# Flamingo gated cross attention: the Q projection moved beside K and V, with shorter lags between the stages

## The reference, cut to what matters

```python
q = (hidden_states @ Wq.T).reshape(bsz, q_len, H, HD).transpose(0, 2, 1, 3)
k = (cross_attention_states @ Wk.T).reshape(bsz, kv_len, KVH, HD).transpose(0, 2, 1, 3)
v = (cross_attention_states @ Wv.T).reshape(bsz, kv_len, KVH, HD).transpose(0, 2, 1, 3)
q = _rmsnorm(q, q_norm_w)
k = jnp.repeat(k, GROUPS, axis=1)
v = jnp.repeat(v, GROUPS, axis=1)
k = _rmsnorm(k, k_norm_w)
scale = 1.0 / np.sqrt(HD)
scores = jnp.einsum('bhqd,bhkd->bhqk', q, k) * scale
scores = scores + attention_mask[:, :, :, :kv_len]
probs = jax.nn.softmax(scores.astype(jnp.float32), axis=-1).astype(q.dtype)
out = jnp.einsum('bhqk,bhkd->bhqd', probs, v)
out = out.transpose(0, 2, 1, 3).reshape(bsz, q_len, H * HD)
return out @ Wo.T
...
base = jnp.einsum('bsd,od->bso', x, W) + bias
return base + lora_out
```

## Time and profile before

| | us |
|---|---|
| median of 3 runs (lowest, highest) | 886.33 (886.28, 888.25) |
| span of the profiled execution, first to last instruction | 882.5 |
| what lies around it, median less span | 3.8 |
| busy: PE, PEld | 830.6, 684.3 |
| busy: DVE, ACT, POOL | 605.8, 416.3, 411.8 |

### The profile page before, as it was taken

How to read it: one execution, slowest core, us unless ns; L and a number is a source line. 1 busy time by engine, 2 the same in 40 slices (tenths; PEclk the granted TensorE clock), 3 DMA queues, 4 the chain that set the end, 5 groups by cost and what they waited for, 6 DMA issues and landing times.

```text
span 882.5 us, 15501 instructions
## 1 busy us (share of the span) xinstructions
PE 830.6 (94%) x4592; PEld 684.3 (78%) x4592; DVE 605.8 (69%) x1710; ACT 416.3 (47%) x1271; POOL 411.8 (47%) x484
## 2 busy tenths in 40 slices
PE   4888889769999999999999999999999999999897
PEld 3555556438888888888888888888888888888786
DVE  5789999633666666676666666666766667666995
ACT  3344444323654455455545545554555455445431
POOL 2566776643553255336435532553363355335532
PEclk9899999889999999999999999999999999999999
DMA  7401000010110011001101100110012010100011
GB/s 262 147 24 30 31 24 13 0 49 24 39 58 25 1 49 61 13 0 48 71 0 48 48 24 0 48 59 12 0 48 71 0 48 24 48 1 13 0 38 59
DMA packets 16947, 34.34 MB, mean 39 GB/s; under 512 B 2320, under 2 KB 2448, under 8 KB 16656
## 3 DMA queue, kind: packets, MB, share of 16 engines
q1 hardware_dynamic: 16912, 33.91, 11.9%
HBM read 31.80 MB, written 2.10 MB: 38 GB/s over the span
## 4 chain that ended last, share of the span: by engine, by line
PE 71%; DVE 3%; issue 2%; POOL 1%; ACT 0%; DVEq 0%; POOLq 0%
PE bank L1122 19%; PE bank L1124 18%; PE bank L1123 18%; PE bank L1210 5%; PE bank L1136 4%; PE bank L1163 3%; PE bank L1138 2%; DVE score L1316 1%; PE bank L1218 1%; POOL rq L1005 1%; PE bank L1226 0%; POOL rk L1001 0%; ACT prob L1050 0%; PE bank L1236 0%; POOL probn L994 0%
## 5 line engine op out<-in xcount | busy, mean ns | idle before, releaser
L994 POOL TENSOR_TENSOR probn<-prob,erec 128x512 f32<-128x512 f32 x64 | 66.8, 1043 | 252.0 <-PE bank L1163 222.4
L1077 ACT ACTIVATE qT_hi<-bank 128x512 fp32r<-128x512 f32 x64 | 38.3, 599 | 161.9 <-PE bank L1124 161.9
L1122 PE MATMUL bank<-nT_hi,wq_hi 128*128 128x512 f32 x256 | 105.2, 411 | 1.8 <-POOL ones L960 1.8
L1122 PE MATMUL bank<-wo_hi,oT_hi 128*128 128x512 f32 x256 | 105.0, 410 | 0.4 <-DVE wq_raw L1373 0.4
L1050 ACT ACTIVATE prob<-score,nmax 128x128 f32<-128x128 f32 x256 | 99.6, 402 | 9.9 <-DVE nmax L1321 9.8
L1124 PE MATMUL bank<-nT_hi,wq_lo 128*128 128x512 f32 x256 | 102.1, 399 | 0.0
L1123 PE MATMUL bank<-nT_lo,wq_hi 128*128 128x512 f32 x256 | 101.9, 398 | 0.0
L1124 PE MATMUL bank<-wo_hi,oT_lo 128*128 128x512 f32 x256 | 100.9, 394 | 0.0
L1123 PE MATMUL bank<-wo_lo,oT_hi 128*128 128x512 f32 x256 | 99.7, 389 | 0.0
L1005 POOL TENSOR_TENSOR rq<-qss,neghalf 128x4 f32<-128x4 f32 x64 | 65.1, 1017 | 50.3 <-DVE qss L1387 50.3
L1381 DVE TENSOR_SCALAR knat<-bank,rk 128x128 f32<-128x128 f32 x64 | 22.4, 350 | 95.4 <-POOL rk L1001 95.4
(11 more groups left out here) (192 smaller groups left out, 2191.8 us busy)
## 6 DMA issues: line engine op xcount, KB each, us to landing
wq_raw<-in_wq SPq DMA_DIRECT2D x32, 256.0 KB, 3.6
wo_raw<-in_wo SPq DMA_DIRECT2D x32, 256.0 KB, 3.0
wkv_raw<-in_wkv SPq DMA_DIRECT2D x8, 512.0 KB, 3.6
ctxn<-in_ctx_n SPq DMA_DIRECT2D x8, 256.0 KB, 2.7
ctxt<-in_ctx_t SPq DMA_DIRECT2D x8, 256.0 KB, 2.7
out<-wkv_raw SPq DMA_DIRECT2D x8, 256.0 KB, 2.0
xres<-in_x SPq DMA_DIRECT2D x1, 1280.0 KB, 11.3
wbase<-in_wbase SPq DMA_DIRECT2D x1, 1024.0 KB, 8.2
```

What stands on the lines that cost most here:

```text
L994: pool.tensor_tensor(probn[:], prob[:], erec[:].unsqueeze(2).broadcast_to([P, HG, P]), ALU.mult).then_inc(normed, 1)
L1077: act.activation(qT_hi[:, s % HG, first * P:(first + 4) * P], q_bank[:], ACT.Copy).then_inc(q_h, 1)
L1122: pe.matmul(out, l_hi, r_hi, start=start, stop=False)
```

## The change

Q is projected token-major too, one batch at a time, with the turned x as the stationary operand and the four heads' weights as the moving one (`project_qkv`), into the PSUM bank beside K and V, so that one tile holds four heads of Q, K and V. ACT squares Q and K together (640 columns), DVE sums them along the row, POOL makes the five inverse norms, DVE scales Q and K together, and PE turns five tiles (`turn_qk`) instead of one. The one-column products and `rq` go; the mask is added and the two score parts are added in one DVE operation each. Per batch there is one slot, with the projection 2 ahead, the turn 1 ahead, probabilities 1 behind and the output projection 2 behind; its addition to x is 3 behind and stands first in DVE's list. The tiles of the cast Wq, Wk and Wv weights are doubled, so that heads alternate. The last stage moves: `fold` stands behind the scores; STAT, NORM and TURN are slots 59, 60 and 62 for batch 0; `turn_batch` and `feed_forward` of one batch stand in the same slot, and `add_batch` stands first in DVE's list of the next. The input wq is laid out accordingly. The loop body has 16 slots. Removed functions are in the listing above; of the new ones these matter:

```diff
-    LAG = 4
     N = G * B
-
-    WQ_SLOT = {2: (0,), 3: (1,), 4: (2,), 5: (3,)}
-    WO_SLOT = {1: (0, 1, 2, 3)}
-
-    LOW_SLOT = {0: (0,), 2: (1,), 3: (2, 3)}
+    RING = 4
+    WKV_AT = 0
+    WQ_AT = {2: (0,), 3: (1,), 4: (2,), 5: (3,)}
+    FOLD = N - B
+    STAT, NORM, TURN = N - B + 3, N - B + 4, N - B + 6
+    LAST = TURN + B - 1
...
+        wkv_hi = wkv_hi + [sb(st, "wkv_hi1", [P, CH * 2 * P], F32R)]
+        wkv_lo = wkv_lo + [sb(st, "wkv_lo1", [P, CH * 2 * P], F32R)]
+        wq_hi = wq_hi + [sb(st, f"wq_hi{c}", [P, D], F32R) for c in range(1, 2 * CH)]
+        wq_lo = wq_lo + [sb(st, f"wq_lo{c}", [P, D], F32R) for c in range(1, 2 * CH)]
...
+        s_bank = pair[0][:].rearrange("p (h i t) -> p h i t", h=HG, i=2)
+        q_bank = bank[2]
+        kv_bank = pair[1][:, HG * P:(HG + 2) * P]
+        qk_bank = pair[1][:, 0:(HG + 1) * P].rearrange("p (h t) -> p h t", h=HG + 1)
+        v_bank = pair[1][:, (HG + 1) * P:(HG + 2) * P]
+        kt_bank = pair[1][:, (HG + 2) * P:(HG + 3) * P]
+        qt_bank, pt_bank, o_bank, y_bank = bank[4:8]
+        t_bank, f_banks = bank[2], (bank[3], bank[4])
...
+        def loops(eng, slot):
+
+            for s in range(-2, B):
+                slot(0, s)
+            with eng.Fori(0, G // 2 - 1) as i:
+                for s in range(B, 3 * B):
+                    slot(i, s)
+            for s in range(N - B, LAST + 2):
+                slot(0, s)
...
+                def project_qkv(i, s, n):
+                    even = parity(s, 2)
+                    here = at(s, 2)
+                    first = (s + 2) % B == 0
+                    need(pe, qk_nat, n)
+                    need(pe, v_h, n)
+                    need(pe, v_l, n)
+                    for c in range(CH):
+                        if first:
+                            need(pe, wq_l, per_head(i, s, 2, CH) - CH + c + 1)
+                        three_pass(q_bank[:], nT_hi[:, c, here], nT_lo[:, c, here],
+                                   wq_hi[even * CH + c][:], wq_lo[even * CH + c][:], c == 0, c == CH - 1)
+                    need(pe, k_l, n)
+                    if first:
+                        need(pe, wkv_l, per_head(i, s, 2, 1))
                     for c in range(CH):
                         w = slice(c * 2 * P, (c + 1) * 2 * P)
...
+                        t = three_pass(kv_bank, cT_hi[:, c, here], cT_lo[:, c, here],
+                                       wkv_hi[even][:, w], wkv_lo[even][:, w], c == 0, c == CH - 1)
+                    t.then_inc(qkv_done, 1)
+
+                def turn_qk(n):
+                    need(pe, qk_nat, n + 1)
+                    need(pe, q_l, n)
+                    need(pe, k_l, n)
                     for h in range(HG):
...
+                        pe.transpose(qt_bank[:, h * P:(h + 1) * P], qkn[:, h, :], ident[:])
+                    pe.transpose(kt_bank, qkn[:, HG, :], ident[:]).then_inc(qk_turned, 1)
...
-                def sum_squares(g, s):
-                    n = B * g + s
-                    need(pe, q_sq, n + LAG + 1)
-                    need(pe, k_h, n + LAG)
-                    need(pe, k_l, n + LAG)
-                    for j in range(4):
-                        t = pe.matmul(ss_bank[:, j:j + 1], qsq[:, j * P:(j + 1) * P], ones[:],
-                                      start=True, stop=True)
-                    t.then_inc(ss_done, 1)
-
-                def turn_k(g, s):
-                    n = B * g + s
-                    need(pe, k_nat, n + LAG)
-                    need(pe, ss_out, n + LAG)
-                    pe.transpose(kt_bank, knat[:], ident[:]).then_inc(kt_done, 1)
...
+                    pe.wait_ge(y_add, n - 2)
...
+                def slot(i, s):
+                    n = 16 * i + s
+                    c, b = chunk(i, s, FOLD), batch(i, s, TURN)
+                    if on(i, s, 0):
+                        scores(n)
                     if c is not None:
...
+                        fold(c, n)
+                    if on(i, s, -1):
+                        turn_probs(n - 1)
+                    if on(i, s, 1):
+                        turn_qk(n + 1)
+                    if on(i, s, 2):
+                        project_qkv(i, s, n + 2)
+                    if b is not None:
+                        turn_batch(b)
+
+                    turns_late = (s - 2) % B == 0
+                    if on(i, s, -2) and not turns_late:
+                        project_out(i, s, n - 2)
+                    if on(i, s, -1):
+                        probs_v(s, n - 1)
+                    if on(i, s, -2) and turns_late:
+                        project_out(i, s, n - 2)
+                    if b is not None:
+                        feed_forward(b)
...
+                def squares(n):
+                    need(act, qkv_done, n + 1)
+                    need(act, qk_ss, n)
+                    act.activation(qksq[:], qk_bank, ACT.Square).then_inc(qk_sq, 1)
+
+                def high_qk(n):
+                    need(act, qk_turned, n + 1)
+                    need(act, s_done, n)
+                    act.activation(kT[:, 0, :], kt_bank, ACT.Copy, scale=wqk[:]).then_inc(k_h, 1)
+                    act.activation(qT_hi[:], qt_bank[:], ACT.Copy).then_inc(q_h, 1)
+
...
+                def slot(i, s):
+                    n = 16 * i + s
+                    b, c = batch(i, s, TURN), chunk(i, s, FOLD + 2)
+                    following = on(i, s, 0) and on(i, s, B)
+                    if on(i, s, -2):
+                        high_out(n - 2)
+                    if on(i, s, -1):
+                        high_probs(n - 1)
+                    if on(i, s, 1):
+                        high_qk(n + 1)
+                    if b is not None:
+                        act.wait_ge(turned, b + 1)
+                        act.activation(tT_hi[:, :, b * P:(b + 1) * P], t_bank[:].rearrange("p (c t) -> p c t", c=CH),
+                                       ACT.Copy).then_inc(t_h, 1)
+                    if following and s % B == WKV_AT:
+                        high_wkv(i, s)
+                    if following:
+                        for k in WQ_AT.get(s % B, ()):
+                            high_wq(i, s, k)
+                    if c is not None:
+                        act.wait_ge(we_sum, c + 1)
+                        act.wait_ge(qkv_done, N - 4)
+                        act.activation(we_hi[:, c, :], w1[:, c, :], ACT.Copy).then_inc(we_h, 1)
+                    if on(i, s, 0):
+                        exponents(n)
+                    if on(i, s, 2):
+                        squares(n + 2)
+                    if on(i, s, 2):
+                        high_v(s, n + 2)
+                    if on(i, s, 0) and s % B == 1:
+                        for h in range(HG):
+                            high_wo(i, s, h)
...
+                def mask_and_max(n):
+                    need(dve, s_done, n + 1)
+                    need(dve, exped, n)
+                    dve.tensor_tensor(score[:], s_bank[:, :, 1, :], maskt[:].unsqueeze(1).broadcast_to([P, HG, P]),
+                                      ALU.add).then_inc(masked, 1)
+                    need(dve, masked, 2 * n + 1)
+                    dve.tensor_tensor(score[:], s_bank[:, :, 0, :], score[:], ALU.add).then_inc(masked, 1)
+                    need(dve, masked, 2 * n + 2)
...
+                def sum_squares(n):
+                    need(dve, qk_sq, n + 1)
+                    need(dve, qk_eps, n)
+                    dve.tensor_reduce(qkss[:], qksq[:], AX.X, ALU.add).then_inc(qk_ss, 1)
...
+                def scale_qk(n):
+                    need(dve, qk_root, n + 1)
+                    need(dve, qk_turned, n)
+                    dve.tensor_tensor(qkn[:], qk_bank, qkr[:].unsqueeze(2).broadcast_to([P, HG + 1, P]),
+                                      ALU.mult).then_inc(qk_nat, 1)
...
+                def slot(i, s):
+                    n = 16 * i + s
+                    b, c = batch(i, s, TURN), chunk(i, s, FOLD)
+                    turns_late = (s - 2) % B == 0
+                    if batch(i, s, TURN + 1) is not None:
+                        add_batch(batch(i, s, TURN + 1))
+                    if on(i, s, -3):
+                        add_out(i, s, n - 3)
+                    if c == 0:
                         dve.wait_ge(ld_d[1], 16)
                         dve.wait_ge(ld_d[2], 16)
                         dve.tensor_scalar(coef[:], lw[:], 2.0, None, ALU.mult).then_inc(coefd, 1)
                         dve.wait_ge(coefd, 1)
                         dve.tensor_scalar(lBc, lBc, coef[:], None, ALU.mult).then_inc(coefd, 1)
+                    if on(i, s, 0):
+                        mask_and_max(n)
+                    if on(i, s, 1):
+                        low_k(n + 1)
+                    if on(i, s, -2) and not turns_late:
+                        low_out(n - 2)
+                    if on(i, s, -1):
+                        low_probs(n - 1)
+                    if on(i, s, 1):
```

(90 more changed lines are left out.)

589 lines of the change are left out of this document (198 added, 391 removed).

## The result

The changed kernel takes 906.36 us (904.52 to 908.98), the kernel before 886.31 in the same session: ratio 1.0233, interval 1.0209 to 1.0258. I had forecast 888.5 with 902 as the upper end, so the time lies outside the range. The profiled execution has a span of 905.3 us and a time of 907.14, 1.8 apart; every run whose span stands beside its time has 1.7 to 2.5 there. The 3.8 that I added back were therefore some 2 us too much: against the forecast span of 884.7 the miss is 20.6, against the forecast median only 17.9, and the smaller figure is luck.

The account below looks back on a forecast made before the run. PE's work alone was taken to bound slots 3 to 56, with waits counting too before and after. Terms -29.4 + 1.1 + 30.5 = +2.2 gave span 884.7, median 888.5; range 876 to 902.

Parts of the forecast that it names:

- The 3.8 that I added back: Whole kernel: median of the runs 886.3 lies 3.8 above the profiled span of 882.5; added to the forecast span.
- The 29.4 us for slots 3 to 56: Middle of the cross attention: 53 slots each 0.555 us shorter, 29.4 us less; bounds 34 to 16 us.
- PE's slot, 9.53: Slots 3 to 56: PE's parts sum to 9.50, with the unexplained 0.02 about 9.53 us a slot.
- rival (d): Slots 3 to 56: PE's slot shrinks less, as if a turn cost 0.15; 13 us more, 902; chance 0.10.
- The norm chain: Slots 3 to 56: squares to scaling of 640 columns take 4.15 us and fit the cover of 4.56.
- Rival (c): Slots 3 to 56: norm chain outgrows its 4.56 us cover, 5.3 us per 0.1 over; 896 to 911; chance 0.12.
- The filling: Before slot 3: every slot waits for the full chain, two gaps cost 2.0 us each; slot 3 at 244.3, 1.1 later.
- my bound of 248.3: Filling: upper bound for the start of slot 3, with the clock cold four times.
- rival (a): Filling and end: clock does not fall in the four gaps taken as cold; 8 us less, 880.5; chance 0.20.
- The end: From slot 56 on: waits on VectorE's queue and cold clock make it 135.3 us against 104.8, 30.5 more.
- Rival (b): Slots 62 to 66: VectorE holds PE up half as long; 7.8 us less, 880.7; chance 0.10.

Follow-up runs that it names:

- 200 against 256 instructions: Changed kernel, loop kept, with 400 waits (200 more PE instructions) or 128 idle turns (256 more) in the filling's PE waits: 900.67 and 903.58 us.
- repeats: Four other kernels with the changed kernel's filling, slot 3 at 245.6, 248.0, 247.6 and 244.2; six with its end, 135.6 to 140.4 us.
- the kernel with the other end: Changed kernel with the last product one slot after its turn, ahead of the output product, and VectorE's addition last in its slot: 885.58 us.
- idle turns: Changed kernel with 100 identity turns that compute nothing on PE in the four waits of the filling: 892.83 us.
- the last kernel: Changed kernel with no loop, other end, 100 idle turns, and VectorE's low part of the attention output ahead of the mask in slots 62 to 65: 865.89 us.

## Why the prediction was wrong

**The missing step: the loop.** The 29.4 us for slots 3 to 56 were 53 times a slot's difference; the longer loop body, which the change itself names, was put at nothing without a reason. It cost 11.3 us in two jumps, more than half of the 20.6 by which the span exceeds the forecast, and no rival covered it. A sum by removed and added operations can't find it: no operation was added. Shown by the kernels without a loop, by the long loop in the old order, and by 200 against 256 instructions. What PE's fetch waits for in the 3.3 us is not in the rows, nor how the start of the body decides whether it waits.

**PE's slot, 9.53, was mis-sized.** It is 9.617, and 0.087 x 53 = 4.6 us. Its parts came out at 0.87 + 0.70 (forecast 1.55 together), 0.91 (0.90), 2.89 (2.86), 1.44 (1.42) and 2.81 (2.77). The parts are 0.01 to 0.04 short each; I had taken them from single rows at the end of the kernel before, and whether that is the reason no run shows. A turn cost 0.101, nine in 0.91, which rules out rival (d) and its 0.15. The 81 ns that the Trainium skill gives, TensorE: Matmul & The Clock Gate, "Back-to-back issue gap", would have been further off. Even so 53 slots gave back 24.8 us without the jumps: this part of the change is a real gain.

**The norm chain held.** Predicted 4.15 us; measured from the end of the K and V matmuls (406.78) to the end of the scaling (410.91) 4.13. The groups with 640 columns were unknown before (page, mean ns of one):

```profile
L1242 DVE TENSOR_REDUCE qkss<-qksq 128x5 f32<-128x640 f32 x64 | 52.6, 822 | 104.2 <-ACT qksq L1139 104.2
L1261 DVE TENSOR_TENSOR qkn<-pair,qkr 128x640 f32<-128x640 f32 x64 | 52.8, 825 | 96.1 <-POOL qkr L1361 96.1
...
L1139 ACT ACTIVATE qksq<-pair 128x640 f32<-128x640 f32 x64 | 45.1, 705 | 82.2 <-PE pair L958 82.2
L1361 POOL TENSOR_TENSOR qkr<-qkse,neghalf 128x5 f32<-128x5 f32 x64 | 76.6, 1196 | 5.6 <-POOL qkse L1358 0.6
```

Predicted 0.71, 0.82, 0.83 and 1.17 by width from the rows of 512 and 4 columns. Rival (c) was no danger.

**The filling: waits right, clock short.** PE waited 4.26, 3.25, 2.78 and 2.09 us for the scaling, as said (4, 3, 3, 2). I had taken the clock as cold behind the first two; it was so behind three. The windows of the changed kernel behind each of the four:

```profile
206.00:210.00 4.00, 3.73 (x13) 3.07 (x14) 1.25 (x3) 0.85 (x2) 0.00 (x0) 0.64 0.00 0
...
218.00:222.00 4.00, 4.00 (x13) 3.10 (x13) 1.93 (x5) 3.27 (x11) 2.19 (x1) 0.65 0.00 2
...
226.00:230.00 4.00, 2.40 (x8) 2.12 (x9) 3.21 (x6) 1.03 (x3) 0.69 (x1) 0.70 0.01 4
...
238.00:242.00 4.00, 3.71 (x20) 3.16 (x21) 3.93 (x8) 3.04 (x12) 4.00 (x4) 1.00 0.44 120
```

A third stretch at 2.0 would be the most of the 2.3 by which slot 3 is late, but that is less than repeats differ: one of them, cold behind the same three waits, starts slot 3 at 244.2, against my 244.3, and another is cold behind the fourth wait too (the window of the kernel with the other end, behind 2.10 us):

```profile
238.00:242.00 4.00, 3.94 (x13) 3.33 (x14) 3.93 (x8) 2.66 (x10) 4.00 (x4) 0.57 0.49 137
```

All of them lie inside my bound of 248.3. With idle turns the windows from 198 to 230 all show 1.00, and slot 3 starts some 5 us earlier, so rival (a) was wrong.

**The end: 137.6 against 135.3.** This term held, and its 2.3 are within the spread of the repeats. Slots 56 to 59 took 45.2 (45.7), 60 and 61 took 9.70 and 10.20 as forecast, slots 62 and 63 with their clock 26.8 (27.7), the rest 45.8 (42.0), where the clock fell after the waits of slots 65 and 66 too (0.59 in 872 to 876, 0.62 in 882 to 886). Rival (b) was wrong: the queue's order held PE up for the full time. The mechanism was right in each slot, and the end that I had priced as the cost of the change could be had 24 us cheaper (113.2 in the last kernel), by two changes of order.

## What to carry to other kernels

When a change makes a loop's body longer, count its instructions per engine and look whether the trace's instruction queue moves anything while the loop runs; if it does, a stall at each jump back and a cold clock behind it are possible and can come and go with code far ahead of the loop, so look for an unexplained PE gap there, or write the loop out. In a queue that runs in order, put what the busiest engine needs next ahead of what only drains, and give a product a slot between its turn and its use. PE's gaps of 3 to 4 us mostly cost again by the clock behind them; in the filling, where the order can't be mended, idle turns in the gap paid.

## What the runs showed of the hardware

A jump back over 1,972 PE instructions stalls PE for 3.2 to 3.5 us, or for 0.1 to 0.3, by where the body starts: 0 and 256 instructions ahead of it stall, 200 do not. Over 2,139 it stalled twice, 2.57 and 2.0 us. Over 1,072 it costs nothing that the rows show (slots of 10.06 and 10.07 on both sides). So a harmless edit far ahead of a loop moved this kernel by 11 us, which an experiment on something else can mistake for its own effect.

The granted clock fell behind PE gaps of 4.26, 3.25 and 2.78 us (0.64 to 0.70 over the next four) and stayed at 1.00 behind one of 2.09; yet in two other kernels it fell behind 2.10 (0.57 and 0.59). A gap of about two us can thus do either. Nor does a long gap always bring it: in one of the repeats it stayed at 1.00 behind the 3.48 us of the second jump. With its stall and its clock a jump over the 1,972 cost 3.7 to 6.7 us in the profiles that stall.
